# Residual added by a diagonal product in PSUM, dt's bias as a row of its product, relu and abs over two tiles

## The reference, cut to what matters

```python
ts, Bm, Cm = (ssm[..., :R], ssm[..., R:R + N], ssm[..., R + N:])   # R = 32, N = 16
ts = rms_forward(ts)
dt = jax.nn.softplus(ts @ W_dt.T + b_dt)                           # 1024 channels
state = state * exp(dt_t * A) + (dt_t * u_t) * B_t                 # a scan over time
...
x = x + ga * attn(h)
h = layernorm(x) * (1 + cb) + sb
x = x + gb * (base + inc * SCALING)                                # the experts' sum
```

## Time and profile before

| | us |
|---|---|
| median of 3 runs | 1601.76 (1599.7 to 1602.21) |
| the profiled execution | 1598.3 |
| its span, first to last instruction | 1596.5 |
| PE busy (matmul) | 1376.4 (86%) |
| DVE busy | 1260.6 (79%) |
| ACT busy | 919.7 (58%) |
| POOL busy | 1078.8 (68%) |

### The profile page before, as it was taken

How to read it: one execution, slowest core, us unless ns; L and a number is a source line. 1 busy time by engine, 2 the same in 40 slices (tenths; PEclk the granted TensorE clock), 3 DMA queues, 4 the chain that set the end, 5 groups by cost and what they waited for, 6 DMA issues and landing times.

```text
span 1596.5 us, 25296 instructions
## 1 busy us (share of the span) xinstructions
PE 1376.4 (86%) x8781; PEld 985.8 (62%) x8781; DVE 1260.6 (79%) x1688; ACT 919.7 (58%) x2465; POOL 1078.8 (68%) x959
## 2 busy tenths in 40 slices
PE   6789999999999588699799789789889979977666
PEld 4567667776776466467557557557656746745543
DVE  5684674556332389989999999999999999999993
ACT  3333342324321666767767777687687687785640
POOL 0353333221322498898998998999899899899970
PEclk9699999999999889799999999999999999999688
DMA  9431321200001200200200110110020030020001
GB/s 337 160 106 35 106 80 55 79 28 27 15 28 32 67 1 1 93 1 1 79 29 1 54 53 1 53 54 1 20 88 1 1 106 1 1 76 18 1 1 40
DMA packets 32531, 77.17 MB, mean 48 GB/s; under 512 B 3810, under 2 KB 4866, under 8 KB 31892
## 3 DMA queue, kind: packets, MB, share of 16 engines
q1 hardware_dynamic: 32404, 75.55, 14.2%
HBM read 66.99 MB, written 8.55 MB: 47 GB/s over the span
## 4 chain that ended last, share of the span: by engine, by line
POOL 18%; DVE 18%; PE 15%; ACT 9%; issue 8%; DVEq 0%; ACTq 0%; POOLq 0%
DVE h L2081 11%; POOL dbu L1906 10%; POOL h L1928 6%; DVE acc L2094 5%; PE ps_h L1422 3%; PE ps_o L1446 3%; ACT ps_a L1629 3%; PE ps_m L1385 1%; PE ps_h L1410 1%; PE ps_m L160 1%; POOL dbu L1910 1%; PE ps_m L162 1%; PE ps_m L161 1%; ACT ab L1714 1%; ACT ab L1733 1%
## 5 line engine op out<-in xcount | busy, mean ns | idle before, releaser
L2081 DVE TENSOR_TENSOR_SCAN h<-ps_a,carry,dbu 128x512 f32<-128x512 f32 x512 | 627.0, 1266 | 18.7 <-ACT carry L1642 7.0
L1906 POOL TENSOR_TENSOR dbu<-dtu,b_all 128x1024 f32<-128x1024 f32 x256 | 604.1, 2360 | 30.3 <-DVE h L2081 16.8
L1629 ACT ACTIVATE ps_a<-dt,a_neg 128x256 f32<-128x256 f32 (+1 forms) x1024 | 444.5, 469 | 152.8 <-DVE h L2081 152.0
L1422 PE MATMUL ps_h<-ident,h 128*128 128x128 f32 x1536 | 230.7, 293 | 128.4 <-DVE acc L2094 114.3
L1422 PEld LDWEIGHTS ps_h<-ident,h 128*128 128x128 f32 x1536 | 182.7, 149 | 186.4 <-DVE h L2081 146.1
L2094 DVE SCALAR_TENSOR_TENSOR acc<-ps_h,c_cur,acc 128x512 f32<-128x512 f32 x384 | 267.6, 737 | 8.0 <-PE ps_h L1422 7.7
L710 POOL TENSOR_TENSOR hid_l<-hid,hid_h 128x256 f16<-128x256 f32 (+1 forms) x88 | 77.2, 880 | 158.4 <-ACT hid_h L601 158.3
L1928 POOL TENSOR_TENSOR h<-h,c_all 128x1024 f32<-128x1024 f32 x64 | 150.9, 2358 | 13.2 <-ACT carry L1642 13.2
L593 ACT ACTIVATE sil<-ps_gu 128x256 f32<-128x256 f32 (+1 forms) x88 | 34.0, 386 | 179.0 <-PE ps_gu L162 179.0
L160 PE MATMUL ps_m<-h_h,wi_h 128*128 128x256 f16 x440 | 122.3, 278 | 6.0 <-PEq L150 2.4
L162 PE MATMUL ps_m<-h_h,wi_l 128*128 128x256 f16 x440 | 121.7, 277 | 0.0
(11 more groups left out here) (345 smaller groups left out, 2846.0 us busy)
## 6 DMA issues: line engine op xcount, KB each, us to landing
b_all<-bt_scratch SPq DMA_DIRECT2D x32, 512.0 KB, 4.1
wm<-in_wmod SPq DMA_DIRECT2D x7, 1024.0 KB, 5.3
wo<-in_wmod SPq DMA_DIRECT2D x5, 1024.0 KB, 10.2
xa<-in_x SPq DMA_DIRECT2D x8, 512.0 KB, 4.5
stage<-in_W_in SPq DMA_DIRECT2D x4, 1024.0 KB
x_scratch<-x SPq DMA_DIRECT2D x8, 512.0 KB, 3.1
c_all<-bt_scratch SPq DMA_DIRECT2D x8, 512.0 KB, 6.1
x<-x_scratch SPq DMA_DIRECT2D x8, 512.0 KB, 3.7
```

The lines of the kernel that those rows point to most:

```text
L1422: tr = pe.transpose(ps_h[:, t, j * P:(j + 1) * P], h[:, s % RING, j, t * P:(t + 1) * P], W["ident"][:])
L1629: ex = nc.scalar.activation(ps_a[:, j, j % 2:], dt[:, m, j % 2:], ACT.Exp, scale=a_neg[:, m, st:st + 1])
L1906: nc.gpsimd.tensor_tensor(dbu[:, s % AHEAD], dtu[:], b_all[:, st, :].unsqueeze(1).to_broadcast([P, DG, CH]), ALU.mult).then_inc(S["db_mul" ...
L2081: nc.vector.tensor_tensor_scan(h[:, s % RING, two].rearrange("p j t -> p (j t)"), ps_a[:, two].rearrange("p j t -> p (j t)"), dbu[:, s % A ...
```

## The change

Three edits:

1. The residual. A new tile `ident_ws` holds 64 times the identity (ACT makes it once). PE adds the product of `ident_ws` and x3 to `ps_o` between the bias row and the product with `mid_t`, and ACT's `base_out` scales the bank by 1/64 into x3, where DVE's `add_experts` did both.
2. dt's bias. `tsb` gets ones in rows 96 to 127 and `w_dt` gets b_dt in row 96, so the product already has the bias; the tile `b_dt` and its load in layer 0 go, a load of one row comes.
3. Relu and abs without bias, over two tiles (512 columns) at a time.

The clearing of `tsb` and the filling of `root` go from POOL to DVE.

```diff
         sp.dma_start(a_neg[:], A["A_log"]).then_inc(S["w1_loaded"], 16)
-        sp.wait_ge(S["pad_done"], 2)
+        sp.wait_ge(S["pad_done"], 1)
         sp.dma_start(w_dt[0:RDT, :], A["W_dt"]).then_inc(S["w1_loaded"], 16)
+        sp.dma_start(w_dt[ONE_ROW:ONE_ROW + 1, :], A["b_dt"]).then_inc(S["w1_loaded"], 16)
...
             pe.matmul(ps_o[:], W["ones"][64:66, 0:P], W["bb"], start=False, stop=False)
+            if p == 0:
+                pe.wait_ge(S["nms_a"], 2)
+            pe.matmul(ps_o[:], ident_ws[:], x3[:, t], start=False, stop=False)
             pe.wait_ge(S["mid_in"], p + 1)
...
-            top = dt[:, m] if m < DG else relu[:, m - DG]
-            nc.scalar.activation(top, dt_bank(m), ACT.Relu, bias=b_dt[:, m:m + 1])
-            nc.scalar.activation(ab[:, m], dt_bank(m), ACT.Abs, bias=b_dt[:, m:m + 1]).then_inc(S["dt_abs"], 1)
+            two = ps_m[:, m // 2 % 2].rearrange("p (k t) -> p k t", k=2)
+            top = dt[:, m:m + 2] if m < DG else relu[:, m - DG:m - DG + 2]
+            nc.scalar.activation(top, two, ACT.Relu)
+            nc.scalar.activation(ab[:, m:m + 2], two, ACT.Abs).then_inc(S["dt_abs"], 2)
...
+        def base_out(p, t):
+            act.wait_ge(S["base_mm"], value(p, TT, t))
+            nc.scalar.activation(x3[:, t], ps_o[:], ACT.Copy, scale=1.0 / WS).then_inc(S["out_done"], 1)
...
+            if p is not None:
+                for q in at_slot(BASE_AT, s):
+                    if q % 2:
+                        base_out(p, q // 2)
...
+        nc.scalar.activation(ident_ws[:], W["ident"][:], ACT.Copy, scale=WS).then_inc(S["nms_a"], 1)
...
-        nc.gpsimd.memset(tsb[:], 0.0).then_inc(S["pad_done"], 1)
-        nc.gpsimd.memset(root[:], ROOT).then_inc(S["pad_done"], 1)
...
-        def add_experts(p, t):
-            dve.wait_ge(S["base_mm"], value(p, TT, t))
-            nc.vector.scalar_tensor_tensor(x3[:, t], ps_o[:], 1.0 / WS, x3[:, t], ALU.mult, ALU.add).then_inc(S["out_done"], 1)
...
+        nc.vector.memset(tsb[0:ONE_ROW, :], 0.0).then_inc(S["begun"], 1)
+        nc.vector.memset(tsb[ONE_ROW:, :], 1.0).then_inc(S["begun"], 1)
+        nc.vector.memset(root[:], ROOT).then_inc(S["begun"], 1)
```

More of the change, by code:

```diff
@@ L121, in build @@
         d_vec = sb("d_vec", [P, KI])
-        b_dt = sb("b_dt", [P, KI])
         expert = sb("expert", [P, NE])
@@ L129, in build @@
              "epsilon": epsilon, "ones": ones, "b_in": b_in, "silu_c": silu_c, "h_h": h_h, "h_l": h_l, "x2": x2,
-             "taps": taps, "d_vec": d_vec, "b_dt": b_dt, "expert": expert, "gb": rows[0:2, :], "cb": rows[32:34, :], "bb": rows[64:66, 0:D], "rb": rb[:], "x2_sum": x2_sum}
+             "taps": taps, "d_vec": d_vec, "expert": expert, "gb": rows[0:2, :], "cb": rows[32:34, :], "bb": rows[64:66, 0:D], "rb": rb[:], "x2_sum": x2_sum}
         W.update(sems("const_loaded wx_loaded mhalf_set bias_done x2_stored met_dve met_pe met_pool"))
@@ L402, in _ @@
         sp.dma_start(W["d_vec"][:], A["D"]).then_inc(W["wx_loaded"], 16)
-        sp.dma_start(W["b_dt"][:], A["b_dt"]).then_inc(W["wx_loaded"], 16)
         sp.dma_start(W["expert"][:], A["expert"]).then_inc(W["wx_loaded"], 16)
@@ L410, in _ @@
         store(LASTK)
-        sp.wait_ge(W["wx_loaded"], 16 * 5)
+        sp.wait_ge(W["wx_loaded"], 16 * 4)
     @block.tensor
@@ L961, in prep @@
             if k == 7 and m == 6:
-                dve.wait_ge(W["wx_loaded"], 16 * 5)
+                dve.wait_ge(W["wx_loaded"], 16 * 4)
                 stepped(nc.vector.tensor_scalar(W["taps"][:], W["taps"][:], 0.5, None, ALU.mult))
@@ L1092, in layer_1 @@
     x3, h3_h, h3_l = W["x2"], W["h_h"], W["h_l"]
-    taps, d_vec, b_dt, expert = W["taps"], W["d_vec"], W["b_dt"], W["expert"]
+    taps, d_vec, expert = W["taps"], W["d_vec"], W["expert"]
     a_neg = sb("a_neg", [P, KI, NS], F32, c)
@@ L1137, in layer_1 @@
     root = sb("root", [P, TT], F32, c)
+    ident_ws = sb("ident_ws", [P, P], F32, c)
     nmr = sb("nmr", [P, TT], F32, c)
@@ L1168, in layer_1 @@
     ROOT = D ** 0.5
+    ONE_ROW = 96
     squares_to = [v[:].rearrange("p k t -> p (k t)")[:, 0:D] for v in (h4_h, h4_l)]
@@ L1591, in _ @@
         turn_tsb(0)
-        pe.wait_ge(S["w1_loaded"], 16 * 2)
+        pe.wait_ge(S["w1_loaded"], 16 * 3)
         for m in range(KI):
@@ L1829, in others @@
                 for m in at_slot(DT_AT, s):
-                    dt_abs(n, m)
+                    if m % 2 == 0:
+                        dt_abs(n, m)
                 if s == 23:
@@ L1865, in _ @@
         squares(0)
-        act.wait_ge(S["w1_loaded"], 16 * 2)
+        act.wait_ge(S["w1_loaded"], 16 * 3)
         nc.scalar.activation(a_neg[:], a_neg[:], ACT.Exp).then_inc(S["aexp_done"], 1)
@@ L1870, in _ @@
         nc.scalar.preload_act_table_set("natural_log_exp_and_others")
+        act.wait_ge(S["begun"], 6)
         tsb_in(0)
-        for m in range(DG):
+        for m in range(0, DG, 2):
             dt_abs(0, m, True)
@@ L1875, in _ @@
         dt_log(0, 0)
-        for m in range(DG, KI):
+        for m in range(DG, KI, 2):
             dt_abs(0, m, True)
         act.wait_ge(S["aneg_done"], 1)
-        act.wait_ge(S["begun"], 3)
         first_decay(0, 0)
@@ L2047, in _ @@
                   .then_inc(S["diag_more"], 1)
-        nc.gpsimd.memset(root[:], ROOT).then_inc(S["pad_done"], 1)
         nc.gpsimd.memset(fold[:, 0:NS, :], 0.0).then_inc(S["fold_done"], 1)
         rms_pow(0)
-        pool.wait_ge(S["begun"], 3)
+        pool.wait_ge(S["begun"], 6)
         pool.wait_ge(S["fold_done"], 1)
-        pool.wait_ge(S["pad_done"], 3)
         iteration(0, None, 1, True)
@@ L2225, in iteration @@
                     choose(p)
[L2226 to L2229, removed]
                 if st == JOIN_AT + 1:
@@ L2305 @@
         "W_x": I["L1_attn_W_x"].T, "W_dt": I["L1_attn_W_dt"].T,
-        "b_dt": I["L1_attn_b_dt"].reshape(KI, P).T,
+        "b_dt": I["L1_attn_b_dt"].reshape(1, DI),
         "A_log": I["L1_attn_A_log"].reshape(KI, P, NS).transpose(1, 0, 2),
```

## The result

The changed kernel takes 1589.65 us (median of 6 runs, 1587.51 to 1590.86) against 1600.82 for the kernel before on the same chip (6 runs, 1596.04 to 1602.21): ratio 0.9931, 95% interval 0.9918 to 0.9945. The forecast was 1592.9 with a range of 1588.5 to 1598.5. The profiled execution took 1589.25, with a span of 1587.5; before it was 1598.3 and 1596.5.

What follows compares the result with a forecast made beforehand. DVE was taken to bound the main loop, with ACT's dt to POOL to ACT to DVE as second bound. Six turns 5.4, last 2.2, start 1.0, first 0.3: 8.9 us off the median 1601.76, so 1592.9 (1588.5 to 1598.5).

Steps and rivals of the forecast that it cites:

- DVE's step: Main loop: removing two add_experts an iteration takes 1.21 us off DVE's queue, 0.84 at step 1 after PE's lateness.
- POOL's chain: ACT's cheaper dt cuts POOL's 1.01 us wait to 0.1; nmr, xn and the scan of step 3 come 0.9 earlier.
- Both chains agree on 0.9: DVE's queue and the path ACT's dt, POOL, ACT, DVE both allow 0.9 us a turn from step 3 on.
- The start: Start of layer 1: dt of chunk 0 gets shorter, so POOL's first product starts 1.0 us earlier.
- The first turn: Chunk 0, no experts behind it: gains only by the path through POOL, 0.3 us (0 to 0.9).
- Six turns: Main loop: six turns each 0.9 us shorter, 5.4 us together.
- The last piece: Last iteration: DVE loses its 1.18 us wait and two times 0.61; gain taken as 2.2 us (1.2 to 2.6).
- (a): Rival: PE becomes the bound of steps 27 to 31, a turn gains 0.4 us, 1595.9 in all; chance 0.15.
- (b): Rival: POOL paces, another wait refills its removed 1.01 us, turns gain nothing, 1598.3 us; chance 0.08.
- (c): Rival: slower, ACT hands the bank back late at step 30, six turns lose 1.1 each, 1604.9 us; chance 0.06.
- (d): Rival: a table load holds ACT 1.38 us longer, a turn loses 0.5, 1601.3 us in all; chance 0.05.

Runs made afterwards that it cites:

- e1_residual: The kernel before with only the residual edit (add_experts off DVE, product and base_out in its place), dt as it was: 1596.86 us, ratio 0.9982.
- e6_nmr_early: The changed kernel with ACT's variance_a ahead of the decays of step 1 and POOL's inv_std_a one step earlier: 1589.51 us, ratio 0.9929 to the kernel before.
- e5_product_twice: The changed kernel with PE's residual product issued twice in each of the 14 places: 1592.77 us, ratio 0.9947 to the kernel before.
- g2_pool_30: The changed kernel with three idle POOL products of 64 columns added at step 30: 1597.26 us, ratio 0.9976 to the kernel before.
- e7_load_later: The changed kernel with ACT's table load moved from step 30 to step 31: 1589.84 us, ratio 0.9927 to the kernel before.

## Why the prediction was right

**The local times.** Forecast and trace are compared by setting the scan of step 29 equal (917.94 in the prediction, 914.46 in the trace, 3.48 apart).

```
                                     forecast, less 3.48   measured
end of the first base_out                 916.3             916.2
end of the second                         923.5             923.6
out_projection(i, 0) starts               923.7             923.7
turn_h of step 31 starts                  925.4             925.5
scan of the next step 0 starts            925.4             925.5
y at step 1                               932.1             932.0
nmr                                       933.2             933.3
scan of step 3                            936.4             936.4
```

Each within 0.1 us: here the method (take a timeline of each engine, move the rows, let each queue run in order) holds, with a row for nearly every duration. ACT's pair came at 0.96, for 0.98 taken. The product's 0.96 for 0.86 was hidden.

**DVE's step** ("2 x 0.61 = 1.21 us an iteration, with DVE saturated there") was right as a removal and wrong as a gain: by itself it gives 0 in a turn (`e1_residual`), since POOL, not DVE, then ends the stretch. The prediction read DVE as "the bound of the main loop" from busy shares, and POOL's as "a second bound"; from `dt_add` to step 3 the order is the other way once DVE is relieved.

**POOL's chain** was the step that made the number: the 1.01 us of wait before `dt_add` went and the turn became 0.92 to 1.03 shorter. "Both chains agree on 0.9" is what the halves show: POOL's limit without the dt edit is 127.1, DVE's limit without the residual edit 126.64, and only with both is it 126.18. But it was put down to nmr, xn and the scan of step 3, which `e6_nmr_early` refutes as the only path: the queue up to `weigh_h` of step 3 is as late. That left the number as it was, since the removed wait is ahead of both.

**Terms of the sum.** The start: POOL's first product 0.97 earlier after `ss_in` (15.28 to 14.31) for 1.0 forecast; run again it was 0.41. The first turn: 0.0 for 0.3 (82.86 and 82.85), and 0.9 when run again. Six turns: 0.34 + 3.92 = 4.3 for 5.4. Four of the turns gave their 0.9, the second 0.34 and one, the longer one of the ledger, 0.25. It loses in two places. DVE waits 0.31 us for POOL's `rms`, which it does not in the usual turn:

```profile
1015.55 0.23 DVE L2139 TENSOR_TENSOR ssn<-ps_s,rms 128x64 f32<-128x64 f32 x1 [0.31 <-POOL rms L1980]
```

POOL is late there because it waited 1.93 us for a carry at 994.11, where it is 1.66 a turn earlier. The other is at step 6, in the usual turn (first row) and in the long one (second):

```profile
950.63 0.69 DVE L2112 TENSOR_TENSOR h_l<-ps_m,h_h 128x512 f16<-128x512 f32 x1 [1.29 <-ACT h_h L1676]
1077.49 0.69 DVE L2112 TENSOR_TENSOR h_l<-ps_m,h_h 128x512 f16<-128x512 f32 x1 [1.65 <-ACT h_h L1676]
```

DVE starts 126.86 us after its turn before, but ACT's `h_h` that it is said to wait for only 126.51 (949.92 and 1076.43), so something else holds DVE for 0.35; what, is open. At step 12 POOL then waits 2.12 us for ACT instead of 1.74. The last piece: 2.6 for 2.2 in the profiled execution, 5.6 when run again. It goes with PE's clock: of its eleven stretches of 20 us the fifth to ninth have 0.65, 0.58, 0.83, 0.74 and 0.83 in the one and 0.66, 0.66, 0.91, 0.66 and 1.00 in the other. That the clock makes all of the 3.0 us between them is not shown. The last iteration's wait of 1.18 us went with its instruction; DVE's next wait there is 0.41:

```profile
1543.61 1.41 DVE L2106 SCALAR_TENSOR_TENSOR acc<-ps_h,c_cur,acc 128x512 f32<-128x512 f32 x2 [0.41 <-PE ps_h L1423]
```

The sum is 7.9 (0.97 + 0.0 + 4.3 + 2.6) for 8.9, and 1.67 more of the profiles' difference belongs to none of the terms: the piece up to the first `ss_in` is 33.41 long in the kernel before, in `e5_product_twice` and in `g2_pool_30`, and 31.74 or 31.75 in all others. In these three profiles some 3 us of it were at half clock, in no other any. The first 6 us of layer 1, in the kernel before and in the changed one (columns as in the earlier trace rows; the clock is the last but two):

```profile
494.00:500.00 6.00, 6.00 (x39) 4.67 (x37) 3.61 (x16) 1.45 (x6) 5.91 (x10) 0.72 0.60 191
```

```profile
494.00:500.00 6.00, 5.79 (x45) 4.92 (x45) 4.33 (x22) 1.86 (x8) 5.76 (x9) 1.00 0.60 210
```

Some of those 6 us were at the lower of the two levels (1.2 GHz) in the one, none in the other; PE was busy all the time in the first.

The time came out 3.3 us below the forecast: 11.2 off the median for 8.9. With the changed kernel's second profile the same four terms sum to 11.6 (0.41 + 0.86 + 4.70 + 5.62), so one profile on each side leaves the sum open by almost 4 us, all of it outside the turns but 0.4. The turns give 4.3 to 4.7 of the 11.2 and are the part that the experiments confirm; that start, first turn and last piece brought the rest, inside the range, owes something to luck. The kernel before has one profile, so its own scatter in these pieces is not known.

**The rivals.** (a) PE as the bound is refuted by `e5_product_twice`. (b) POOL does pace part of the turn, but the wait was not refilled: after the change POOL has the same three waits at the same length (1.77, 1.92 and 1.66 us; before 1.77, 1.94 and 1.65). (c) did not occur: `base_out` came as forecast. (d): the load ends at 922.94 and `base_out` starts at 922.96. By the Trainium skill's "ScalarE: Activation LUTs", section "What ACT_TABLE_LOAD costs", a DRAIN of about 1380 ns goes with a switch; this trace again shows none behind it, and `e7_load_later` has nothing to gain from moving it.

## What to carry to other kernels

With several engines near saturation, follow the chain that ended last through one whole turn and note which engine's queue it runs through in which steps. In this kernel an operation was worth its length in such a place and nothing in the other that was tried, whatever the busy shares say. Test the reading with an operation of known length, since the chain names one path and another may be as late. Two edits that relieve two engines side by side can be worth 0 and 0.46 alone and 0.92 together, so an edit that gives nothing by itself is not to be thrown away before its partner is tried. Where turns repeat within about 0.1 us, the length of a turn in one profile tells more than times of single executions that scatter by 3 us and more.

## What the runs showed of the hardware

DVE's product of 64 columns with both operands in SBUF lasts 0.23 us (the shortest), but 1.80 in the median of 24 and up to 2.28 beside POOL's products (one line's instructions: ns min/median/max):

```profile
L2231 DVE TENSOR_TENSOR spare<-ident x24: 226/1803/2275, 593.8 to 1516.8; 128x64 f32<-128x64 f32 x24
```

The first starts at 854.38 within a POOL product that ends at 856.11 and lasts until 856.19; the second, between two of POOL's, takes 0.23; the third lasts 2.27 and ends at 858.76, right behind POOL's next product (858.68). In the first turn, where POOL has nothing after 595.18, the three take 1.15, 0.23 and 0.23. The kernel's own long DVE instructions have an operand in PSUM (the scan `ps_a`, `add_state` `ps_h`), and keep their lengths beside POOL (1.27 us a scan). By the Trainium skill's "SBUF — State Buffer", section "SBUF: two separate sides", a DVE operation with two SBUF inputs and a GpSimd (POOL) operation that reads SBUF shut each other out for a whole instruction; this trace agrees, with 1.8 to 2.3 us for 0.23. A small fp32 operation with both operands in SBUF, moved from POOL to DVE in such a kernel, can be dear.

DVE's fill of 96 x 256 took 0.27 us, that of 32 x 256 as much, and POOL's of the whole tile 0.46; a copy of 512 columns out of PSUM costs ACT 0.57 to 0.60, alone or among others.
